# Edge stage of a two-layer graph kernel: split rows turned by DMA transposes instead of TensorE turns, four banks for the first products

## The reference, cut to what matters

```python
x = _layernorm(x + L0(x, edge_index, node_vec, ...), axis=-1)
# layer 1, per head:
feats = jnp.maximum(x @ w1 + bb1, 0.0) @ w2 + bb2
x_cat = jnp.concatenate([feats[row], feats[col], elem[:, None]], axis=1)
hid = jnp.maximum(x_cat @ a1 + aab1, 0.0)
e1 = leaky_relu((hid @ a2 + aab2)[:, 0], 0.2)
w = jnp.exp(e1 - jnp.max(e1))
pooled = segment_sum(w[:, None] * feats[col], row, n)
out = pooled / (segment_sum(w, row, n) + 1e-10)[:, None]
x = _layernorm(x + transpose(out), axis=-1)
```

## Time and profile before

| | us |
|---|---|
| median of three runs | 3220.41 |
| lowest, highest | 3213.28, 3221.02 |
| the profiled execution | 3212.97 |
| its span in the trace | 3211.2 |

### The profile page before, as it was taken

The page is one execution under the profiler, slowest core; times in us unless marked ns, Lnnn a source line. Parts: engine busy times, 40 slices in busy tenths (PEclk is TensorE's granted clock), DMA queues, the critical chain, the costliest instruction groups (busy, mean ns, idle before and its releaser), DMA issues. The chain is left out here.

```text
span 3211.2 us, 58166 instructions
## 1 busy us (share of the span) xinstructions
PE 2942.0 (92%) x15789; PEld 1796.1 (56%) x15789; DVE 2572.9 (80%) x8853; ACT 1848.4 (58%) x4205; POOL 1770.5 (55%) x1692
## 2 busy tenths in 40 slices
PE   5888999799999958999999999999999999985774
PEld 4555666466666634555555555555555655553442
DVE  7999998655555577888888888888888888878995
ACT  3444554355555525666666666666666666655885
POOL 2776577577777735544454445444444544403776
PEclk9999999899999979999999999999999999997997
DMA  5888997465665645555555555555555555525884
GB/s 168 277 275 277 331 315 247 148 208 195 203 204 192 208 142 175 188 180 180 196 179 182 187 196 177 181 191 192 178 181 195 183 180 186 195 80 197 286 275 148
DMA packets 343600, 648.29 MB, mean 202 GB/s; under 512 B 43230, under 2 KB 250762, under 8 KB 343462
## 3 DMA queue, kind: packets, MB, share of 16 engines
q1 hardware_dynamic: 261174, 411.39, 38.0%
q0 software_dynamic: 75744, 232.45, 22.6%
q10 hardware_dynamic: 6544, 2.89, 0.4%
HBM read 338.64 MB, written 322.05 MB: 206 GB/s over the span
## 5 line engine op out<-in xcount | busy, mean ns | idle before, releaser
L1188 POOL TENSOR_TENSOR u_hc<-u_hc 128x1536 f32<-128x1536 f32 x98 | 270.2, 2757 | 661.8 <-DVE u_h L1350 467.8
L993 PE MATMUL bank<-w_node,xT 128*128 128x384 f32 x1564 | 565.2, 490 | 26.1 <-ACT bank L611 26.1
L1505 PE MATMUL bank<-xh,w1h 128*128 128x512 f16 x1568 | 469.5, 381 | 16.8 <-ACT hidT L1265 6.0
L1505 PE MATMUL bank<-xh,w1l 128*128 128x512 f16 x1568 | 468.2, 380 | 0.0
L1505 PE MATMUL bank<-xl,w1h 128*128 128x512 f16 x1568 | 468.2, 380 | 0.0
L1265 ACT ACTIVATE hidT<-bank,b1c 128x512 f32<-128x512 f32 x392 | 268.9, 686 | 332.4 <-PE bank L1505 297.1
L1371 DVE TENSOR_SCALAR hidT<-bank,b1c 128x512 f32<-128x512 f32 x392 | 294.2, 750 | 188.9 <-PE bank L1505 188.8
L611 ACT ACTIVATE bank<-bias_all 128x512 f32<-128x512 f32 x391 | 234.1, 599 | 313.6 <-DVE H L704 313.2
L993 PEld LDWEIGHTS bank<-w_node,xT 128*128 128x128 f32 x1564 | 280.0, 191 | 175.6 <-ACT bank L611 29.3
L1319 ACT ACTIVATE o_row<-h_row,row_nb,row_r 128x256 f32<-128x256 f32 x390 | 222.2, 593 | 270.3 <-DMA h_row<-hc_tab 270.3
L1520 PE MATMUL bank<-hidT,w2f 128*64 128x256 f32 x3136 | 360.1, 381 | 7.5 <-issue 2.0
(11 more groups left out here) (293 smaller groups left out, 6003.5 us busy)
## 6 DMA issues: line engine op xcount, KB each, us to landing
hc_tab<-H SPq DMA_DIRECT2D x78, 960.0 KB
er<-edge_tab SPq DMA_DIRECT2D x98, 512.0 KB, 4.5
X<-in_x SPq DMA_DIRECT2D x78, 640.0 KB
h_row<-hc_tab SPq DMA_DIRECT2D x97, 512.0 KB, 7.8
out_x<-o_row SPq DMA_DIRECT2D x97, 512.0 KB, 2.8
hc_tab<-zero_row SPq DMA_DIRECT2D x10, 4032.0 KB
hc_tab<-zero_row SPq DMA_DIRECT2D x9, 3840.0 KB
edge_tab<-u_x SPq DMA_DIRECT2D x98, 256.0 KB, 4.5
```

Source lines behind the costliest of these rows:

```text
L993: ins = t_.matmul(p[:, 0:384], xT[t // 2 % XR][:, t % 2, c * P:(c + 1) * P], w_node[:, c, :], start=False, stop=c == 1, skip_group_check=True)
L1188: g.tensor_tensor(c, c, u_hc[s][:, :, MULT:MULT + 3].unsqueeze(3).to_broadcast([P, 4, 3, P]), ALU.mult).then_inc(u_scaled, 1)
L1505: ins = t_.matmul(bank[2 + m % 2][:, :], w[:, c, m * P:(m + 1) * P], xx[s][:, c, :], start=n == 0, stop=n == 5)
```

## The change

`turn` leaves TensorE. `high` now reads the rows `u_x` in SBUF (one 128x1024 instruction in place of two of 128x512 out of PSUM) and writes `eh`, edge-major; `low` likewise writes `el` from `u_x` and `eh`, both in SBUF. SyncE turns each of them with one DMA transpose of 128x1024 float16 (256 KB) into `xh` and `xl`. `turn_h(u)` waits for `high(u)` and until all eight products of round u-2, which read the same `xh`, are finished; `turn_l(u)` likewise. The matmuls read `xh` with a step of 256 elements between their four groups of 128 columns. Banks 0 and 1 are free now, and the `hidden` products go round four banks (2, 3, 0, 1), so that each waits for the relu of four products earlier. `high` moves to the same step as `norm`, behind `relu_4` and ahead of `norm_o_2` and `seed_1`; `low` moves to directly behind `stat`. Apart from that, step counters of VectorE are merged into one semaphore, and the last stage reuses semaphores of this one.

```diff
 class Steps:
-    def __init__(self, eng, sem):
-        self.eng, self.sem, self.base, self.n = eng, sem, 0, 0
+    def __init__(self, eng, sem, base=0):
+        self.eng, self.sem, self.base, self.n = eng, sem, base, 0
...
-        xh = [tmp(f"xh{s}", [P, 2, 512], F16) for s in range(2)]
-        xl = [tmp(f"xl{s}", [P, 2, 512], F16) for s in range(2)]
+        eh = [tmp(f"eh{s}", [P, 4 * D], F16) for s in range(2)]
+        el = tmp("el", [P, 4 * D], F16)
+        xh = [tmp(f"xh{s}", [P, 8, P], F16) for s in range(2)]
+        xl = [tmp(f"xl{s}", [P, 8, P], F16) for s in range(2)]
+        HB = (2, 3, 0, 1)
...
             def _(sp):
+                def turn_h(u, s):
+                    sp.wait_ge(t_high, u + 1)
+                    if after(u, 2):
+                        sp.wait_ge(w1_ready, u * 8 - 8)
+                    sp.sem_inc(sp_hop, 1)
+                    sp.dma_start_transpose(xh[s][:, :, :], eh[s][:, :]).then_inc(h_turned[s], 16)
+
+                def turn_l(u, s):
+                    sp.wait_ge(t_low, u + 1)
+                    if after(u, 2):
+                        sp.wait_ge(w1_ready, u * 8 - 8)
+                    sp.sem_inc(sp_hop, 1)
+                    sp.dma_start_transpose(xl[s][:, :, :], el[:, :]).then_inc(l_turned[s], 16)
...
-                skewed(sp, US, 2, [(keep_f, 4), (keep_o, 4), (keep_x, 0), (load_h, 2)])
+                skewed(sp, US, 2, [(keep_o, 4), (turn_l, 1), (keep_f, 4), (keep_x, 0), (turn_h, 0), (load_h, 2)])
...
                 def norm(u, s):
                     act.wait_ge(v_nb, u + 1)
                     if after(u, 2):
-                        act.wait_ge(t_ready, u - 1)
+                        act.wait_ge(t_low, u - 1)
...
                 def high(u, s):
-                    act.wait_ge(t_ready, u + 1)
+                    act.wait_ge(v_x, u * 4 + 4)
                     if after(u, 2):
-                        act.wait_ge(w1_ready, u * 8 - 8)
-                    for c in range(2):
-                        a.activation(xh[s][:, c, :], bank[c][:, :], ACT.Copy, scale=X_UP).then_inc(t_high, 1)
+                        act.wait_ge(h_turned[s], (u - s) * 8)
+                    a.activation(eh[s][:, :], u_x[s][:, :, :].rearrange("p k d -> p (k d)"), ACT.Copy, scale=X_UP)\
+                        .then_inc(t_high, 1)
...
-                                    (features_1, 3), (root, 0), (relu_2, 2), (norm, 0), (relu_4, 2), (norm_o_2, 3),
-                                    (seed_1, 3), (high, 1), (norm_o_3, 3), (relu_6, 2)])
+                                    (features_1, 3), (root, 0), (relu_2, 2), (norm, 0), (relu_4, 2), (high, 0),
+                                    (norm_o_2, 3), (seed_1, 3), (norm_o_3, 3), (relu_6, 2)])
...
                 def low(u, s):
-                    for c in range(2):
-                        dve.wait_ge(t_high, u * 2 + (c + 1))
-                        v.scalar_tensor_tensor(out=xl[s][:, c, :], in0=bank[c][:, :], scalar=X_UP,
-                                               in1=xh[s][:, c, :], op0=ALU.mult, op1=ALU.subtract)\
-                            .then_inc(t_low, 1)
+                    dve.wait_ge(t_high, u + 1)
+                    if after(u, 1):
+                        dve.wait_ge(l_turned[1 - s], (u + s) * 8)
+                    v.scalar_tensor_tensor(out=el[:, :], in0=u_x[s][:, :, :].rearrange("p k d -> p (k d)"),
+                                           scalar=X_UP, in1=eh[s][:, :], op0=ALU.mult, op1=ALU.subtract)\
+                        .then_inc(t_low, 1)
...
-                skewed(dve, US, 2, [(stat, 0), (feat_1, 4), (relu_1, 2), (scale, 0), (feat_0, 3), (relu_3, 2),
-                                    (dots_0, 3), (relu_5, 2), (low, 1), (dots_1, 3), (relu_7, 2)])
+                skewed(dve, US, 2, [(stat, 0), (low, 1), (feat_1, 4), (relu_1, 2), (scale, 0), (feat_0, 3), (relu_3, 2),
+                                    (dots_0, 3), (relu_5, 2), (dots_1, 3), (relu_7, 2)])
...
-                def turn(u, s):
-                    pe.wait_ge(v_x, u * 4 + 4)
...
                 def hidden(u, s, m):
                     if m == 0:
-                        pe.wait_ge(t_low, u * 2 + 2)
+                        pe.wait_ge(h_turned[s], (u - s) * 8 + 16)
...
-                    if m > 1 or after(u, 1):
-                        pe.wait_ge(act_hid if m % 2 == 0 else dve_hid, u * 4 + m // 2)
+                    if m > 3 or after(u, 1):
+                        pe.wait_ge(act_hid if m % 2 == 0 else dve_hid, u * 4 + (m // 2 - 1))
                     n = 0
                     for w, xx in ((w1h, xh), (w1l, xh), (w1h, xl)):
+                        if m == 0 and xx is xl:
+                            pe.wait_ge(l_turned[s], (u - s) * 8 + 16)
                         for c in range(2):
-                            ins = t_.matmul(bank[2 + m % 2][:, :], w[:, c, m * P:(m + 1) * P], xx[s][:, c, :],
+                            ins = t_.matmul(bank[HB[m % 4]][:, :], w[:, c, m * P:(m + 1) * P],
+                                            xx[s][:, :, :].rearrange("p (k c) e -> p c k e", c=2)[:, c, :, :],
                                             start=n == 0, stop=n == 5)
...
-                                   (hidden_3_4, 1), (turn, 0), (hidden_5, 1), (scores_1, 2), (hidden_6, 1),
-                                   (hidden_7, 1)])
+                                   (hidden_3_4, 1), (hidden_5, 1), (scores_1, 2), (hidden_6, 1), (hidden_7, 1)])
```

More of the change, by code:

```diff
@@ L200, in build @@
         dve1 = sem("dve1")
+        dve_at = [0]
         act1 = sem("act1")
         act_hop = sem("act_hop")
-        pool_hop, dve_hop = sem("pool_hop"), sem("dve_hop")
+        pool_hop, dve_hop, sp_hop = sem("pool_hop"), sem("dve_hop"), sem("sp_hop")
         pc = [0]
@@ L363, in _ @@
                 st.wait()
+                dve_at[0] = st.base + st.n
             @block.tensor
@@ L456, in build @@
         deg_all = tmp("deg_all", [P, 2])
-        tab_ready, dve3 = sem("tab_ready"), sem("dve3")
+        tab_ready = sem("tab_ready")
         xg_in = [sem(f"xg_in{q}") for q in range(RS // 2)]
@@ L686, in _ @@
                 v = nc.vector
-                st = Steps(dve, dve3)
+                st = Steps(dve, dve1, dve_at[0])
                 def first(t, i):
@@ L1132, in build @@
         w_down = tmp("w_down", [P, MB])
-        dve4, w_turned, up_ready, up_rows, rows_read, w1_scaled = (sem(n) for n in (
-            "dve4 w1_turned w1_up_ready w1_up_rows w1_rows_read w1_scaled").split())
+        w_turned, up_ready, up_rows, rows_read, w1_scaled = (sem(n) for n in (
+            "w1_turned w1_up_ready w1_up_rows w1_rows_read w1_scaled").split())
         hidT = [tmp(f"hidT{m}", [P, 512]) for m in range(8)]
@@ L1153, in build @@
         opened_s, s_seeded = sem("scores_opened"), sem("scores_seeded")
-        names = ("v_stat v_mv v_sd v_r v_nb v_x t_ready t_high t_low w1_ready act_hid dve_hid w2_ready "
+        names = ("v_stat v_mv v_sd v_r v_nb v_x t_high t_low w1_ready act_hid dve_hid w2_ready "
                  "cat_ready f_ready a_ready at_read dots_done sc_done").split()
-        (v_stat, v_mv, v_sd, v_r, v_nb, v_x, t_ready, t_high, t_low, w1_ready, act_hid, dve_hid, w2_ready,
+        (v_stat, v_mv, v_sd, v_r, v_nb, v_x, t_high, t_low, w1_ready, act_hid, dve_hid, w2_ready,
          cat_ready, f_ready, a_ready, at_read, dots_done, sc_done) = (sem(n) for n in names)
         x_out = [sem(f"x_out{s}") for s in range(2)]
+        h_turned = [sem(f"h_turned{s}") for s in range(2)]
+        l_turned = [sem(f"l_turned{s}") for s in range(2)]
         f_out = [sem(f"f_out{s}") for s in range(2)]
@@ L1610, in build @@
         fix_at = tmp("fix_at", [P, 1], I32)
-        (dve5, mx_ready, mxa_ready, sub_done, w_ready, den_ready, val_ready, agg_ready, pick_ready, head_used,
+        (mx_ready, mxa_ready, sub_done, w_ready, den_ready, val_ready, agg_ready, pick_ready, head_used,
          tail_ready, z_ready, zst, zmv, zvar, zsd, zr, znb, zo_ready, fix_x_in, at_ready, sums_ready,
          fvar, fsd, fnb, fo_ready, fo_out) = (sem(n) for n in (
-             "dve5 mx_ready mxa_ready sub_done w_ready w_den_ready val_ready agg_ready pick_ready head_used "
+             "mx_ready mxa_ready sub_done w_ready w_den_ready val_ready agg_ready pick_ready head_used "
              "tail_ready z_ready z_stat z_aggr z_var z_sd z_r z_nb zo_ready fix_x_in fix_at_ready sums_ready "
              "fix_var fix_sd fix_nb fix_o_ready fix_o_out").split())
-        er_in = [sem(f"er_in{s}") for s in range(RING)]
+        er_in = x_out + f_out + h_in
+        ER0 = US // 2 * 16
         z_opened, z_seeded = sem("z_opened"), sem("z_seeded")
@@ L1705, in _ @@
                 v = nc.vector
-                st = Steps(dve, dve5)
+                st = Steps(dve, dve1, dve_at[0])
                 st.done(v.memset(goes_back[:, 0:1], 0.0))
```

20 lines of the change are left out of this document (6 added, 14 removed).

## The result

The changed kernel takes 3561.28 us (median of four runs, 3555.57 to 3568.86), the kernel before 3217.37 us in the same comparison: a ratio of 1.107, 95% interval 1.106 to 1.109. Forecast were 3555 us, with a range of 3330 to 3880.

The account below looks back on a forecast made before the run. TensorE's own work was taken as the bound, 16.95 us a round; the loop through `load_h` sums to 20.4, and 97 rounds x (20.4 - 16.95) plus 3 us of fill led to 3555 us, range 3330 to 3880.

Parts of the forecast that it names:

- The load behind the transpose: SyncE: `load_h` queued behind `turn_h` closes a loop of 20.4 us per round; TensorE waits some 2.8 us ahead of `scores_0`.
- The transpose's transfer: SyncE's DMA queue, directly ahead of `load_h`'s data: 1.3 us taken, with ends of 0.74 and 3.7.
- The cast ahead of the seed: ScalarE: `high`, taken as 1.0 us, delays `seed_1`; TensorE stalls 1.76 us at `scores_1` every round, bounds 1.4 and 2.8.
- `low` behind `stat`: VectorE: `low` or `gate`'s second part waits about 1 us; cost nothing, 0.5 us a round if the cover is gone.
- the cover: VectorE's room in a round: busy 14.5 us, with 1 us more still below 17.6.
- Turns gone, four banks: TensorE: saves 0.87 us of turns and 0.2 of waits for relus a round, giving 15.9 us in place of 16.95.
- GpSimd's loop: GpSimd, `gate` and gathers: 11.9 and 5.1 us make 17.0 a round, limiting the faster case, whose chance was 0.03.
- Fill and end: First round of the edge stage: transposes in series ahead of `hidden_0` cost about 3 us, once.
- the upper bound: Transpose's transfer in pieces of 256 bytes: 1024 pieces, 64 on each of 16 engines at 0.058 us, 3.7 us.
- its lower bound: Transpose's transfer of 256 KB at a copy's rate, 355 GB/s: 0.74 us.

Follow-up runs that it names:

- e1: Changed kernel with `load_h` ahead of `turn_h` in SyncE's list, all else the same: 3295.39 us, ratio 1.025 to the kernel before.
- e12: Kernel before, without transposes, `load_h` on SyncE held back until the round's last product has finished: 3281.10 us, ratio 1.021.
- e2: Changed kernel with `high` behind `seed_1` on ScalarE, SyncE's list unchanged: 3558.42 us, ratio 1.108 to the kernel before.
- e5: e2 with `hidden_2`'s six products computed twice in every round, to fill TensorE's wait: 3452.26 us, ratio 1.075 to the kernel before.
- e6: Changed kernel with `hidden_2`'s products computed twice, the same edit as e5: 3546.46 us, ratio 1.104 to the kernel before.
- e3: Changed kernel with both `load_h` ahead of `turn_h` and `high` behind `seed_1`: 3251.26 us, ratio 1.012 to the kernel before.
- e8: Changed kernel with `low` directly behind `scale` on VectorE and nothing else: 3558.39 us, ratio 1.109 to the kernel before.
- e7: e3 with `low` directly behind `scale` on VectorE and `turn_l` behind `keep_f` on SyncE: 3214.51 us, ratio 1.000 to the kernel before.
- e9: e7 with `seed_1` ahead of `norm_o_2` on ScalarE: 3194.40 us, ratio 0.993 to the kernel before.

## Why the prediction was right

**The load behind the transpose.** Right in mechanism and size; e1 gives back 266 of 344 us, where 2.8 us x 97 = 272 were expected of it. The terms, from the round shown:

| term, us | forecast | measured |
|---|---|---|
| last product's end to `load_h`'s issue | 1.67 | 1.79 |
| issue to `norm_o_0`, transpose ahead | 3.6 + 1.3 | 4.12 |
| `norm_o_0` to `scores_0` | 3.8 | 3.79 |
| `scores_0` to the end of `hidden_7` | 10.03 | 10.19 |
| sum | 20.4 | 19.9 here, 20.3 in the mean |

The transpose's transfer was over-sized in the loop. Its issue takes 1.24 us (1.2 was taken). The load landed in 4.3 us in the median behind it, in 3.6 in e12 without it: 0.7 us, not 1.3, as if a part of the transfer were over when the load goes out. TensorE's wait ahead of `scores_0` is 2.25 us in the mean, where 2.8 was forecast.

**The cast ahead of the seed.** 1.76 us forecast, 1.59 measured; the cast takes 1.05 us (1.0 taken). But only a part of it is the cast's. With the cast back behind the seed 0.65 us are left (e2, e5), because TensorE, without its turns, asks for the seed 0.87 us sooner; the prediction's own terms give 3.06 - 1.0 - 1.30 = 0.76 for this, and it put the whole 1.76 under the cast. e6 against e5 gives 94 us for the cast, e1 against e3 only 44: in e3 `low` ahead of `scale` keeps the stall at 1.1 us.

**`low` behind `stat`.** The wait beside `gate` came as forecast (2.12 us in place of 1.23, `gate`'s second part 2.03 in place of 1.27), and its price of nothing held for the changed kernel (e8). It was not nothing as such: "cost nothing, 0.5 us a round if the cover is gone" is what e7 then showed, 37 us or 0.4 us a round. The way was another than VectorE's share, by which the prediction judged: `scale`, and behind it ScalarE's `norm`, `relu_4` and `seed_1`, wait in the queue behind `low`.

**Turns gone, four banks.** 0.87 us a round of TensorE left the kernel, and its waits for banks with them. The gain appears only in e9, and there as 0.3 us a round (1300 / 78 = 16.7 against 16.95). Most rounds of e9 take 16.5 us with 0.41 us of stall, so TensorE's order without it is 16.1; 15.9 was forecast. The 17.0 us that the prediction gave GpSimd's loop as a limit are no limit: 11.9 and 5.1 are the two parts of one round before, waits included, and add up to its length whatever sets it.

**Fill and end.** Too small: 3 us forecast. From the stage's first DMA to the first load of the last stage it is 2070.5 us after against 1724.8 before, 346 more, of which 97 rounds x 3.3 = 322; some 24 us are fill and end. SyncE's and TensorE's timelines after show the most of it:

```profile
1208.77 1.24 SPq L1224 DMA_TRANSPOSE xl<-el  x1
```

```profile
1211.10 1.03 PE L1520 MATMUL bank<-xh,w1h 128*128 128x512 f16 x2 [18.86 <-DMA xh<-eh]
...
1218.00 1.04 PE L1520 MATMUL bank<-xl,w1h 128*128 128x512 f16 x2 [5.02 <-DMA xl<-el]
```

The first transpose of `el` was issued at 1208.77, beside the first gathers, and TensorE could go on at 1218.00, 9.2 us later; in the steady rounds it lands in 3.1 us. That the total came out within 6 us rests in part on luck, on errors of opposite sign: 97 rounds 0.13 us shorter than forecast (13 us less), fill and end 21 us longer, and 5 us more in the node stage, where only the sharing of semaphores was changed.

**The transposes' share of the DMA engines.** The DMA view of the changed kernel, 1450 to 2950 us (packets, MB and the share of 16 engines' time; then an issue with its count and the median us to landing):

```profile
q1 hardware_dynamic: 244329, 153.73, 37.5%
...
xh<-eh SPq DMA_TRANSPOSE x74, 3.1
```

Per round that is 0.375 x 1500 x 16 / 74 = 121.6 us of one DMA engine, before 0.261 x 1390 x 16 / 82 = 70.8; the two transposes add 50.8, or 1.6 us of all sixteen each, 165 GB/s. This is an estimate, which takes the time of all other packets as unchanged; the same sum gives 183 GB/s in e1 (41.5% of 1300 us, 74 rounds) and 132 in e8 (41.4%, 64 rounds). The packets rise from 1215 to 3302 a round, 1043 for each transpose: pieces of 256 bytes, as the upper bound had assumed, but at 0.024 us each instead of 0.058. "DMA: Bandwidth & Descriptors" of the Trainium skill, in its table of latency and other measured facts, gives 261 GB/s to a DMA transpose with a non-contiguous middle; the traces, with 132 to 183 by this estimate, do not agree, and they decide. The copies' 355 GB/s, from which the prediction took its lower bound, is not reached either.

## What to carry to other kernels

Where a DMA that waits for the end of a round is put into an issuing queue, look at the next DMA in that queue and at what waits for it: an unrelated load of side work became a loop of 20 us here, and moving it by one place gave back 266 of 344 us. An instruction that is added on an engine with room still has a place, and what is queued behind it decides its price, not the engine's share. When removing one of two waits gains nothing, look at the granted clock before dropping the theory.

## What had not been expected of the hardware

- In e2 a wait of TensorE of 2.28 us in a round of some 20.9 us was followed by the lower clock for about 3 us, and so were 43 of 64 such waits; in the changed kernel, where the mean is 2.25 us and a second wait of 1.59 us follows, only 12 of 63 were. The length of this wait alone doesn't decide it: ahead of the slow rounds of the changed kernel it was 1.95 to 2.49 us, ahead of the others 1.80 to 2.81. Filling 1.3 us of the wait with repeated products brought the clock to 1.00 and 106 us back. Which of the differences between the kernels decides it stays open.
- A DMA transpose of 128x1024 float16 took 1.24 us of SyncE's issue, and 3.1 us from issue to landing in the median of the changed kernel, 9.6 at most. With `low` and its transpose behind `scale` the median for `xl` was 5.3 (e7) and 5.8 us (e8).
- `low`, an operation of VectorE with both inputs in SBUF, took 2.1 to 4.5 us in place of 1.2 beside GpSimd's `gate`, and `gate`'s second part 2.03 in place of 1.27: each holds up the other.
